# GpSimd in place of ScalarE makes the bfloat16 copy of the adjacency, a step ahead of its use

## The chip, the cores and the metric

The kernel runs on 1 core of one Trainium2 chip. The metric is device time in microseconds of one execution. In this text PE is TensorE, DVE is VectorE, ACT is ScalarE, POOL is GpSimd and SP is SyncE, whose queue issues most of the loads.

## What is computed

The input x has 128 graphs of 128 nodes with 128 features; adj holds for each graph a 128x128 matrix of small integers. Cut to what matters:

```python
h = layernorm(x)
e_k = leaky_relu(einsum('bid,bjd->bij', h * a_k, h), 0.2)     # k = 0..3
alpha = where(adj == k + 1, e_k, alpha)                       # from -9e15, for k = 0..3
x = x + softmax(alpha) @ h
# then, on layernorm(x): 16 experts, top 2 of each token,
# silu(x @ w1[e]) * (x @ w2[e]) @ w3[e], weighted by the gates, added to x
```

## The kernel before

The kernel has two stages. The first walks over the graphs in 32 groups of 4 (T = 4, C = 512 columns) and does the attention and the gating; it ends by sending each token's row to a list in DRAM, sorted by expert. The second reads those lists in tiles of 256 rows and multiplies them with the experts' weights, once for each of the two experts of a token. It isn't touched by the change.

The first stage is written by hand as a software pipeline. `steps(step)` calls a function `step(s, on)` for s = −1 to 33 on each engine, and `on(lag)` is true while group s − lag exists. So in step s the engines work on different groups: the layer norm of group s + 1 (`on(-1)`), the transposed copies and the scores' mask of group s (`on(0)`), its scores on PE a step later (`on(1)`), the softmax (`on(2)`), the new rows (`on(3)`) and the gating (`on(4)`, `on(5)`). Each engine runs its list in order, and semaphores tie them together. What matters here, by engine, in a step s:

- ACT: the first two of the four mask planes, as squares of the adjacency (L677), the copies hT and hTa from PSUM (L685, L687), four exponentials with their sums (L695), then `adjb`, the bfloat16 copy of the adjacency of group s + 1 (L703), x1T (L667), probT (L710), and h of group s + 1 (L716), which waits for the norms (`s_sh`).
- DVE: the maximum of the four scores (L931), statistics of x for group s + 1 (L815), leaky relu (L947), the scaled logits (L846), new rows (L884), the other two mask planes from `adjb` (L966), more statistics (L815) and the top two (L903, L907).
- POOL: `stamp` (two small copies, L545 and L547), `norms_of` (four instructions, L554, L557, L563 with a power, L567), `second_gates` every other step (L573), and from step 7 on `send`, four indirect DMAs of 128 rows each (L581).
- SP: `load_adj` (L387) into one of two int32 buffers, after the squares of two groups before (`s_squares`), `load_x` (L382) into one of six, after the new rows that free it (`s_x1`), and up to step 17 the weights of an expert (`load_expert`).

Before, `adjb` is a single buffer, so ACT writes it for group s + 1 only after DVE has made the mask of group s (`s_pen`). All these areas are slices of one tensor, late, and so the trace calls them late; a row is told by its line.

Of the kernel before, what the change touches and what calls it, by code (L numbers as in the profile page):

```python
# [5 lines left out]
def gnn_then_moe(nc: bass.Bass, x, adj, a0, a1, a2, a3, gate_w, gate_b, w1, w2, w3, out):  # L6
# [7 lines left out]
    f32, bf16, i32, u32, u16 = (mybir.dt.float32, mybir.dt.bfloat16, mybir.dt.int32, mybir.dt.uint32,  # L14
                                mybir.dt.uint16)
# [6 lines left out]
    K = 4  # L22
    T = 4
    G = B // T
    C = T * D
# [3 lines left out]
    ROOT = 2.0 ** 28  # L29
# [49 lines left out]
    with ctx:  # L79
# [18 lines left out]
        score = late[:, K * C:(K + 1) * C]  # L98
        prob = late[:, (K + 1) * C:(K + 3) * C].rearrange("p (q c) -> p q c", q=2)
        adjt = late[:, (K + 3) * C:(K + 5) * C].bitcast(i32).rearrange("p (q c) -> p q c", q=2)  # L100
        adjb = late[:, (K + 5) * C:(K + 6) * C].bitcast(bf16)[:, 0:C]
        pen = late[:, (K + 6) * C:(2 * K + 6) * C].bitcast(bf16).rearrange("p (q k c) -> p q k c", q=2, k=K)
        minusb = sb("minusb", [P, P], bf16)

# [203 lines left out]
        def wait(eng, s, value):  # L308

            if not isinstance(value, int) or value > 0:  # L310
                eng.wait_ge(s, value)
# [13 lines left out]
        def pair(s, lag):  # L325

            return (s - lag) // 2 if 0 < s - lag < G and (s - lag) % 2 else None
# [51 lines left out]
        def _(sp):  # L379
# [4 lines left out]

            def load_adj(g):
                wait(sp, s_squares, g - 1)
                sp.dma_start(adjt[:, g % 2, :].rearrange("p (t d) -> p t d", t=T),  # L387
                             adj_v[:, ds(g * T, T), :]).then_inc(s_adj[g % 2], 16)

# [118 lines left out]
        def _(pool):  # L508
# [41 lines left out]
            def norms_of(s):  # L550
                ln, b = norms(s), s % 2
                wait(pool, s_st1, min(s + 2, G))
                wait(pool, s_st2, s - 3)
                nc.gpsimd.tensor_scalar(veps[:, b, ln, :], stats[:, b, ln, :, 2], 1.0 / D, EPS, ALU.mult, ALU.add  # L554
                                        ).then_inc(s_ve, 1)
                wait(pool, s_sh, s + 1)
                nc.gpsimd.tensor_scalar(negmean[:, ln, :], stats[:, b, ln, :, 1], -1.0, None, ALU.mult  # L557
                                        ).then_inc(s_neg, 1)
                pool.wait_ge(s_ve, s + 2)
                wait(pool, s_h, min(s, G))  # L560
                wait(pool, s_scaled, s - 5)
                wait(pool, s_dest, 2 * (s - 6) + 2)
                nc.gpsimd.tensor_tensor(norm[:, b, ln, :, 0], veps[:, b, ln, :], minus_half[:, ln, :],  # L563
                                        ALU.pow).then_inc(s_rs, 1)
                pool.wait_ge(s_rs, s + 2)
                pool.wait_ge(s_neg, s + 2)
                nc.gpsimd.tensor_tensor(norm[:, b, ln, :, 1], negmean[:, ln, :], norm[:, b, ln, :, 0], ALU.mult  # L567
                                        ).then_inc(s_sh, 1)
# [7 lines left out]
            def send(g, some=range(T)):  # L576
# [3 lines left out]
                for t in some:  # L580
                    pool.indirect_dma_start(  # L581
                        first_list[:, :], bass.IndirectOffsetOnAxis(ap=slot[:, g % SB, t:t + 1], axis=0),
                        stage_v(g % SB)[:, t, :], None).then_inc(s_scat[g % SB], 16)

            def step(s, on):
                if on(5):
                    stamp(s)
                norms_of(s)
                if pair(s, 6) is not None:
                    second_gates(pair(s, 6))  # L590
                if s >= 7 and s <= G:
                    send(s - 7)
# [62 lines left out]
        def _(act):  # L655
# [13 lines left out]
            def step(s, on):  # L669
                b = s % 2  # L670
                if pair(s, 6) is not None:
                    second_gate(pair(s, 6))
                if on(0):
                    act.wait_ge(s_adj[s % 2], (s // 2 + 1) * 16)
                    wait(act, s_S, s - 1)
                    for k in range(SQUARES):
                        last = nc.scalar.activation(pen[:, s % 2, k, :], adjt[:, s % 2, :], ACT.Square,  # L677
                                                    scale=ROOT, bias=shift[:, k:k + 1])
                    last.then_inc(s_squares, 1)
                if s == 0:  # L680
                    act.wait_ge(s_small, 6 * 16)
                if on(0):
                    act.wait_ge(s_hTp, s + 1)
                    wait(act, s_S, s - 1)
                    nc.scalar.activation(hT[:, s % 2, :], psT[:, :], ACT.Copy)  # L685
                    for k in range(K):
                        last = nc.scalar.activation(hTa[s % 2][:, k, :], psT[:, :], ACT.Copy, scale=acol[:, k:k + 1])  # L687
                    last.then_inc(s_hT, 1)
                if on(2):
                    g, p = s - 2, s % 2  # L690
                    act.wait_ge(s_nm, g + 1)
                    wait(act, s_rinv, g - 1)
                    for t in range(T):
                        c = slice(t * D, (t + 1) * D)
                        last = nc.scalar.activation(prob[:, p, c], prob[:, p, c], ACT.Exp,  # L695
                                                    bias=negmax[:, p, t:t + 1],
                                                    accum_out=rowsum[:, p, t:t + 1])
                    last.then_inc(s_prob, 1)
                if on(-1):
                    g = s + 1  # L700
                    act.wait_ge(s_adj[g % 2], (g // 2 + 1) * 16)
                    wait(act, s_pen, g)
                    nc.scalar.activation(adjb, adjt[:, g % 2, :], ACT.Copy).then_inc(s_adjb, 1)  # L703
                if on(4):
                    new_rows_turned(s - 4)
                if on(2):
                    g = s - 2
                    act.wait_ge(s_probTp, g + 1)
                    wait(act, s_O, g)
                    nc.scalar.activation(probT[:, :], psO[:, :], ACT.Copy).then_inc(s_probT, 1)  # L710
                if on(-1):
                    g = s + 1
                    act.wait_ge(s_sh, s + 2)
                    wait(act, s_O, g - HB + 1)
                    for t in range(T):
                        last = nc.scalar.activation(h[:, g % HB, t * D:(t + 1) * D], X[:, g % XQ, t * D:(t + 1) * D],  # L716
                                                    ACT.Identity, scale=norm[:, b, 0, t, 0:1],
                                                    bias=norm[:, b, 0, t, 1:2])
                    last.then_inc(s_h, 1)
# [46 lines left out]
        def _(dve):  # L766
# [157 lines left out]
            def step(s, on):  # L924
# [37 lines left out]
                if on(0):  # L962
                    dve.wait_ge(s_adjb, s + 1)
                    wait(dve, s_S, s - 1)
                    for k in range(SQUARES, K):
                        last = v.tensor_scalar(pen[:, s % 2, k, :], adjb, float(k + 1), ROOT * ROOT,  # L966
                                               ALU.not_equal, ALU.mult)
                    last.then_inc(s_pen, 1)
                if on(3):
# [362 lines left out]
```

## Time and profile before

| | us |
|---|---|
| median of 3 runs | 868.1 (863.27 to 870.77) |
| the profiled execution | 869.26 |
| its span | 867.5 |
| first stage: SP's first load of a list (L446) | at 308.87 |
| POOL busy in the span | 516.5 |
| ACT busy in the span | 416.0 |
| DVE busy in the span | 502.6 |
| PE busy in the span | 732.3 |

A row of the timeline gives the start and the duration in us, the engine, the line of the kernel, the operation, what it writes and reads, and in square brackets the time in which its engine stood idle ahead of it and what ended that. Durations overlap a little, since an engine begins the next instruction before the last one's writes are done, so starts are compared with starts. The profiled execution took 1.8 us more than its span.

### The profile page before, as it was taken

Reading aid. Unit: us, or ns where it says so; the run is one execution under the profiler, and the core shown is the slowest. Engines: PE = TensorE matmul, PEld = TensorE weight load, DVE = VectorE, ACT = ScalarE, POOL = GpSimd, SP = SyncE. Lnnn points to the kernel's source line nnn. Section 1 sums busy time; section 2 is a strip of 40 time slices with the busy share of each in tenths; the row PEclk is TensorE's granted clock in tenths of the full one; section 3 lists DMA queues with packets and bytes.
Section 4 is the critical chain, followed back from the end, with each engine's and each line's share of the span. In section 5 each row is a group of like instructions: output and inputs, shape, how many; then the busy total and the mean of one; then the engine's idle time right before and its main releaser. Section 6 shows DMA issues by size and latency. Waiting matters only on the chain.

```text
span 867.5 us, 17419 instructions
## 1 busy us (share of the span) xinstructions
PE 732.3 (84%) x4422; PEld 588.2 (68%) x4423; DVE 502.6 (58%) x1706; ACT 416.0 (48%) x1011; POOL 516.5 (60%) x670
## 2 busy tenths in 40 slices
PE   4899999999999756888887888886979897988985
PEld 2465656656565645777776888776867787987874
DVE  2899999999999863545444444442433333343332
ACT  7999999999999321222222222222322222222220
POOL 3337777878777766455554554554455554545545
PEclk9999999999999967999999898998999998999998
DMA  5233545332321144776665555534876665566640
GB/s 158 71 112 112 158 121 158 100 104 83 103 85 41 33 152 151 210 232 221 215 224 187 178 176 167 191 122 145 269 214 189 186 192 185 182 183 193 192 140 8
DMA packets 127463, 133.29 MB, mean 154 GB/s; under 512 B 16362, under 2 KB 98545, under 8 KB 127378
## 3 DMA queue, kind: packets, MB, share of 16 engines
q1 hardware_dynamic: 107008, 94.66, 36.6%
q0 software_dynamic: 15616, 34.38, 11.6%
q10 hardware_dynamic: 4754, 3.25, 1.2%
q8 instruction: 36, 0.59, 0.3%
q14 instruction: 49, 0.40, 0.2%
HBM read 52.28 MB, written 41.19 MB: 108 GB/s over the span
## 4 chain that ended last, share of the span: by engine, by line
PE 44%; DVE 23%; issue 16%; another core or an unknown queue 10%; ACT 4%; POOL 1%; DMA 1%; SPq 0%; DVEq 0%; ACTq 0%; POOLq 0%
PE psS L1256 24%; PE bank L1281 14%; PE bank L1271 4%; DVE stage L884 3%; DVE stats L815 3%; DVE late L931 3%; DVE bestix L907 2%; DVE late L947 2%; DVE X L1081 1%; ACT late L687 1%; DVE best L903 1%; DVE late L966 1%; DVE xin L1090 1%; PE psS L1164 1%
## 5 line engine op out<-in xcount | busy, mean ns | idle before, releaser
L1256 PE MATMUL psS<-X,late 128*128 128x256 f32 (+1 forms) x1280 | 262.6, 354 | 3.3 <-issue 3.3
L1081 DVE TENSOR_TENSOR X<-silu,psS 128x512 f32<-128x512 f32 x144 | 98.7, 686 | 225.6 <-remote 132.0
L1256 PEld LDWEIGHTS psS<-X,late 128*128 128x128 f32 x1280 | 212.0, 202 | 22.8 <-issue 3.9
L734 ACT ACTIVATE silu<-psS 128x512 f32<-128x512 f32 x144 | 86.0, 597 | 281.2 <-remote 143.5
L630 POOL DMA_INDIRECT second_list<-xin x144 | 142.1, 987 | 126.0 <-DVE xin L1090 82.4
L641 POOL DMA_INDIRECT out_dram<-xin x144 | 141.7, 984 | 120.7 <-DVE xin L1090 77.4
L1281 PE MATMUL bank<-wts,X 128*128 (+1 forms) x1152 | 164.6, 288 | 36.8 <-DVE X L1081 28.5
L1281 PEld LDWEIGHTS bank<-wts,X 128*128 128x128 f32 x1152 | 147.2, 200 | 46.4 <-issue 46.2
L581 POOL DMA_INDIRECT first_list<-stage,slot x128 | 127.9, 1000 | 52.5 <-issue 41.1
L1090 DVE SCALAR_TENSOR_TENSOR xin<-bank,xin 128x128 f32<-128x128 f32 x288 | 87.5, 345 | 96.7 <-remote 63.3
L1164 PE MATMUL psS<-late,hT 128*128 128x512 f32 x256 | 118.2, 604 | 3.1 <-ACT late L687 2.8
L739 ACT ACTIVATE X<-bank 128x256 f32<-128x256 f32 x144 | 55.2, 383 | 128.0 <-remote 72.0
L1271 PE MATMUL bank<-ident,xin 128*128 128x128 f32 x288 | 58.6, 288 | 44.7 <-issue 39.7
L1271 PEld LDWEIGHTS bank<-ident,xin 128*128 128x128 f32 x288 | 38.8, 148 | 62.5 <-issue 54.8
L1164 PEld LDWEIGHTS psS<-late,hT 128*128 128x128 f32 x256 | 46.9, 194 | 50.1 <-issue 47.2
L931 DVE TENSOR_REDUCE late<-psS 128x512 f32<-128x2048 f32 x32 | 72.9, 2279 | 12.6 <-PE psS L1169 12.1
L687 ACT ACTIVATE late<-bank,acol 128x512 f32<-128x512 f32 x128 | 77.6, 705 | 0.0
L563 POOL TENSOR_TENSOR norm<-veps,minus_half 128x8 f32<-128x8 f32 (+1 forms) x37 | 56.5, 1526 | 0.0
L716 ACT ACTIVATE h<-X,norm 128x128 f32<-128x128 f32 x128 | 53.4, 518 | 1.2 <-POOL norm L567 1.2
L695 ACT ACTIVATE late<-late,negmax 128x128 f32<-128x128 f32 x128 | 50.5, 427 | 6.5 <-DVE negmax L954 6.5
L987 DVE TENSOR_SCALAR xin<-xin 128x128 f32<-128x128 f32 x144 | 44.0, 351 | 0.0
L677 ACT ACTIVATE late<-late,shift 128x512 bf16<-128x512 int32 x64 | 43.4, 742 | 0.0
(156 smaller groups left out, 821.1 us busy)
## 6 DMA issues: line engine op xcount, KB each, us to landing
late<-wts SPq DMA_DIRECT2D x160, 256.0 KB
xin<-second_list SPq DMA_DIRECT2D x48, 262.0 KB
X<-in_x_dram SPq DMA_DIRECT2D x32, 256.0 KB
late<-in_adj_dram SPq DMA_DIRECT2D x32, 256.0 KB
xin<-first_list SPq DMA_DIRECT2D x48, 134.0 KB
xin<-second_list SPq DMA_DIRECT2D x48, 131.0 KB
wts<-in_L_ffn_w_dram SPq DMA_DIRECT2D x48, 128.0 KB
xin<-first_list SPq DMA_DIRECT2D x48, 67.0 KB
```

The costliest lines, as they stand in the source:

```text
L581: pool.indirect_dma_start(first_list[:, :], bass.IndirectOffsetOnAxis(ap=slot[:, g % SB, t:t + 1], axis=0), stage_v(g % SB)[:, t, :], None ...
L630: pool.indirect_dma_start(second_list[:, :], bass.IndirectOffsetOnAxis(ap=xin[:, at, k, SLOT1:SLOT1 + 1].bitcast(i32), axis=0), xin[:, at, ...
L641: pool.indirect_dma_start(out_rows[:, :], bass.IndirectOffsetOnAxis(ap=xin[:, at, k, DEST:DEST + 1].bitcast(i32), axis=0), xin[:, at, k, 0 ...
L687: last = nc.scalar.activation(hTa[s % 2][:, k, :], psT[:, :], ACT.Copy, scale=acol[:, k:k + 1])
L734: nc.scalar.activation(silu[:, u % 2, :], psG[u % 2], ACT.Silu).then_inc(s_silu[u % TURNS], 1)
L931: v.tensor_reduce(score.rearrange("p (t d) -> p t d", t=T), psS[:, :, :].rearrange("p t (k d) -> p t d k", k=K), AX, ALU.max).then_inc(s_s ...
L1081: v.tensor_tensor(hid[:, u % HIDS, :], silu[:, u % 2, :], psU[u % 2], ALU.mult).then_inc(s_hid[u % TURNS], 1)
L1090: last = v.scalar_tensor_tensor(at, psY[k % 2][:, t * D:(t + 1) * D], xin[:, k, t, GATE[r]:GATE[r] + 1], at, ALU.mult, ALU.add)
L1164: mm(psS[:, t, :], hT[:, g % 2, t * D:(t + 1) * D], hTa[g % 2][:, :, t * D:(t + 1) * D], start=True, stop=False)
L1256: last = mm(out[:, c * W2 + rows.start:c * W2 + rows.stop], at[:, half * H + c * P:half * H + (c + 1) * P], xT[:, u % XTS, rows], start=Tr ...
L1271: last = nc.tensor.transpose(psX[k % 2][:, t * P:(t + 1) * P], xin[:, k, t, ROW:ROW2], ident[:, :])
L1281: last = mm(psY[k % 2][:, t * D:(t + 1) * D], hid[:, k % HIDS, at:at + P], wts[:, ds(e[t] * EW + (UP + c * D), D)], start=(c == 0), stop=( ...
```

## The change

POOL makes the copy, as the first work of its step s for group s + 1, into one of two buffers; for group 0 it follows the norms of step −1. ACT's activation goes. `load_adj` waits in addition for the copy of two groups before, since POOL now reads the int32 buffer too. DVE reads the buffer of its group's parity. The two bfloat16 buffers lie where the one lay, in the half of its area that was not used.

```diff
-        adjb = late[:, (K + 5) * C:(K + 6) * C].bitcast(bf16)[:, 0:C]
+        adjb = late[:, (K + 5) * C:(K + 6) * C].bitcast(bf16).rearrange("p (q c) -> p q c", q=2)
...
             def load_adj(g):
                 wait(sp, s_squares, g - 1)
+                wait(sp, s_adjb, g - 1)
...
+            def small_adjacency(g):
+                pool.wait_ge(s_adj[g % 2], (g // 2 + 1) * 16)
+                wait(pool, s_pen, g - 1)
+                nc.gpsimd.tensor_copy(adjb[:, g % 2, :], adjt[:, g % 2, :]).then_inc(s_adjb, 1)
+
             def step(s, on):
+                if on(-1) and s >= 0:
+                    small_adjacency(s + 1)
                 if on(5):
                     stamp(s)
                 norms_of(s)
+                if s < 0:
+                    small_adjacency(0)
...
-                if on(-1):
-                    g = s + 1
-                    act.wait_ge(s_adj[g % 2], (g // 2 + 1) * 16)
-                    wait(act, s_pen, g)
-                    nc.scalar.activation(adjb, adjt[:, g % 2, :], ACT.Copy).then_inc(s_adjb, 1)
                 if on(4):
                     new_rows_turned(s - 4)
...
-                        last = v.tensor_scalar(pen[:, s % 2, k, :], adjb, float(k + 1), ROOT * ROOT,
+                        last = v.tensor_scalar(pen[:, s % 2, k, :], adjb[:, s % 2, :], float(k + 1), ROOT * ROOT,
                                                ALU.not_equal, ALU.mult)
```

On POOL one step of the first stage, with its row sends, stands like this before (stage is the area of the rows to be sent, veps, negmean and norm are the norm's values; the names behind "waits" are semaphores):

```order
L545 COPY stage<-dest 128x4 [waits s_sh]
L547 COPY stage<-norm 128x4x2
L554 TENSOR_SCALAR veps<-stats 128x8 [waits s_st2,s_st1]
L557 TENSOR_SCALAR negmean<-stats 128x8 [waits s_sh]
L563 TENSOR_TENSOR norm<-veps,minus_half 128x8 [waits s_scaled,s_dest,s_h,s_ve]
L567 TENSOR_TENSOR norm<-negmean,norm 128x8 [waits s_neg,s_rs]
L573 TENSOR_TENSOR stage<-e,stage 128x8 [waits s_g1]
```

and like this now (the lines have moved by one, and CAST is the new copy):

```order
L589 CAST late<-late 128x512 [waits s_pen,s_adj0]
L546 COPY stage<-dest 128x4 [waits s_sh]
L548 COPY stage<-norm 128x4x2
L555 TENSOR_SCALAR veps<-stats 128x8 [waits s_st2,s_st1]
L558 TENSOR_SCALAR negmean<-stats 128x8 [waits s_sh]
L564 TENSOR_TENSOR norm<-veps,minus_half 128x8 [waits s_scaled,s_dest,s_h,s_ve]
L568 TENSOR_TENSOR norm<-negmean,norm 128x8 [waits s_neg,s_rs]
L574 TENSOR_TENSOR stage<-e,stage 128x8 [waits s_g1]
```

Everything else of POOL's step now stands behind the copy and its two waits. On ACT the same place before, from the exponentials to h:

```order
L695 ACTIVATE late,rowsum<-late,negmax 128x128 [waits s_rinv,s_nm]
L695 ACTIVATE late,rowsum<-late,negmax 128x128 x3
L703 ACTIVATE late<-late 128x512 [waits s_pen,s_adj1]
L667 ACTIVATE x1T<-bank 128x512 [waits s_L,s_x1Tp]
L710 ACTIVATE probT<-bank 128x512 [waits s_O,s_probTp]
L716 ACTIVATE h<-X,norm 128x128 [waits s_O,s_sh]
```

and now:

```order
L705 ACTIVATE late,rowsum<-late,negmax 128x128 [waits s_rinv,s_nm]
L705 ACTIVATE late,rowsum<-late,negmax 128x128 x3
L677 ACTIVATE x1T<-bank 128x512 [waits s_L,s_x1Tp]
L715 ACTIVATE probT<-bank 128x512 [waits s_O,s_probTp]
L721 ACTIVATE h<-X,norm 128x128 [waits s_O,s_sh]
```

The copy between the exponentials and x1T is gone, and nothing else has moved.

## Rows read from the trace of the kernel before

**Rows 1.** Busy time of each engine, 100 to 260 us, with instruction counts.

```profile
core 0: us, PE busy (x) PEld busy (x) DVE busy (x) ACT busy (x) POOL busy (x), PEclk, DMA share, GB/s
...
100.00:260.00 160.00, 148.72 (x812) 96.24 (x811) 154.27 (x596) 156.79 (x407) 126.39 (x192) 1.00 0.37 109
```

**Rows 2.** Timeline of POOL: step 8, three steps in the middle, step 31.

```profile
73.30 0.20 POOL L545 COPY stage<-dest 128x4 int32<-128x4 int32 x1
...
200.01 0.20 POOL L567 TENSOR_TENSOR norm<-negmean,norm 128x8 f32<-128x8 f32 x1
...
205.65 0.54 POOL L545 COPY stage<-dest 128x4 int32<-128x4 int32 x1
...
209.85 1.15 POOL L581 DMA_INDIRECT first_list<-stage,slot  x1 [0.82 <-POOL stage L573]
211.30 0.96 POOL L581 DMA_INDIRECT first_list<-stage,slot  x1 [0.30 <-issue]
...
214.80 0.46 POOL L545 COPY stage<-dest 128x4 int32<-128x4 int32 x1
...
223.37 0.21 POOL L545 COPY stage<-dest 128x4 int32<-128x4 int32 x1
...
276.47 0.20 POOL L545 COPY stage<-dest 128x4 int32<-128x4 int32 x1
```

**Rows 3.** The stamp's copy in ns (min/median/max), and DVE beside POOL.

```profile
L545 POOL COPY stage<-dest x32: 191/452/606, 41.8 to 319.2; 128x4 int32<-128x4 int32 x32
...
46.91 0.68 DVE L947 SCALAR_TENSOR_TENSOR late<-late 128x512 f32<-128x512 f32 x1
47.08 0.56 POOL L554 TENSOR_SCALAR veps<-stats 128x8 f32<-128x8 f32 x1 [4.98 <-DVE stats L815]
...
205.47 0.68 DVE L947 SCALAR_TENSOR_TENSOR late<-late 128x512 f32<-128x512 f32 x1
206.66 0.23 DVE L846 TENSOR_TENSOR scaled<-bank,norm 128x64 f32<-128x64 f32 x1 [0.52 <-remote]
```

**Rows 4.** Timeline of ACT and PE from the last exponential's sum to h.

```profile
202.30 0.21 ACT L695 ACTIVATION_READ_ACCUMULATOR late<-late,negmax 128x1 f32 x1
202.39 0.63 ACT L703 ACTIVATE late<-late 128x512 bf16<-128x512 int32 x1
202.56 0.66 PE L1179 MATMUL bank<-ident,late 128*128 128x128 f32 x4 [0.57 <-issue]
202.91 0.60 ACT L667 ACTIVATE x1T<-bank 128x512 f32<-128x512 f32 x1
203.39 0.61 ACT L710 ACTIVATE probT<-bank 128x512 f32<-128x512 f32 x1
203.87 1.66 ACT L716 ACTIVATE h<-X,norm 128x128 f32<-128x128 f32 x4
```

**Rows 5.** Timeline of ACT in step 2.

```profile
28.38 0.60 ACT L710 ACTIVATE probT<-bank 128x512 f32<-128x512 f32 x1 [0.23 <-PE bank L1179]
```

**Rows 6.** Timeline of POOL's constants at the start of the kernel.

```profile
1.33 0.54 POOL L516 MEMSET padding<- 128x524 f32 x1
...
3.04 0.20 POOL L532 MEMSET unit<- 1x128 bf16 x1
3.21 0.28 POOL L533 TENSOR_SCALAR_AFFINE_SELECT ident<-ident 128x128 f32<-128x128 f32 x1
3.46 0.28 POOL L535 TENSOR_SCALAR_AFFINE_SELECT lower<-ones 128x128 bf16<-128x128 bf16 x1
```

**Rows 7.** Timeline: POOL's norms of step 31 and DVE's scaled logits of step 32.

```profile
278.49 0.20 POOL L567 TENSOR_TENSOR norm<-negmean,norm 128x4 f32<-128x4 f32 x1
...
285.31 0.22 DVE L846 TENSOR_TENSOR scaled<-bank,norm 128x64 f32<-128x64 f32 x1
```

**Rows 8.** Load of an adjacency, DMA engines busy in 40 slices of 100 to 110 us, POOL's step 12.

```profile
105.27 0.48 SPq L387 DMA_DIRECT2D late<-in_adj_dram  x1
...
DMA  4000000000000000015699995656689999528000
...
108.52 0.45 POOL L545 COPY stage<-dest 128x4 int32<-128x4 int32 x1
```

## The prediction

> **What bounds the kernel now.** I read the busy times by stage first [rows 1]. The change touches only the first stage; the expert tiles behind it keep their code, so they can only start earlier or later. In its steady part, 100 to 260 us, ACT is busy 156.8 of 160 us, DVE 154.3, PE 148.7. POOL shows 126.4, which looks like room. It isn't: the timeline of POOL [rows 2] shows each step's work back to back. The step that begins at 205.65 us is followed by the next at 214.80 and 223.37. Within it nothing waits for another engine; the holes are fixed ones of 0.30 us ahead of each row send (0.8 or 0.5 ahead of the first), which the view calls "issue". They are part of the cost of sending, so POOL's real load is a whole step. From 73.30 us (step 8) to 276.47 us (step 31) 23 steps take 203.2 us, 8.83 each: ACT, DVE and POOL all have about one step of work per step.
>
> What part of POOL's step could give way? Only the first copy of a step, the stamp from dest: its shortest is 0.19 us, its median 0.45 [rows 3]. The reason is in the same group: it starts at 205.65 while DVE runs L947, an instruction with two inputs, and ends at 206.19, just behind DVE's 206.15. The norm chain's first instruction shows the same, 0.56 us instead of 0.20 at 47.08, beside L947 from 46.91 to 47.59. So some 0.26 us a step, 23 × 0.26 = 6.0 us, is stretching and not work. POOL alone would need 203.2 − 6.0 = 197.2 us for these steps, 8.57 each. DVE pays too: L846 starts 0.5 us late at 206.66.
>
> **ACT's part: what is removed.** One activation of 0.65 us a step, start to start 0.52 (202.39 to 202.91), 31 of them besides the first. The trap is what stands around it [rows 4]. The last exponential's sum ends at 202.51. PE can transpose only then, 202.56 to 203.22, and the probability copy L710 needs that. L703 and L667 fill this very hole. Without L703, L667 runs at 202.4 to 203.0, and L710 goes at about 203.24 instead of 203.39. So 0.15 us a step is won, not 0.52. In steps 2 and 3 there is no L667, and L710 waits for PE even now [rows 5]: nothing is won. Only the steps before the first exponential win the whole 0.5. Up to step 7: 0.5 + 4 × 0.15, say 1 us.
>
> **POOL's part: what is added.** One conversion of 128x512 int32 to bf16 ahead of all other work of each step. No row shows it. The nearest is AFFINE_SELECT, which reads and writes 128 elements, 0.25 us start to start (3.21 to 3.46) [rows 6]. If only what exceeds a fixed 0.17 us (the 1x128 memset at 3.04, start to start) grows with size, 512 elements take 0.17 + 4 × 0.08 = 0.5 us; if all of it grows, 1.0 us. The fill of 524 elements took 0.54 without reading anything, so much below 0.5 is out, and a gain from the copy itself is excluded, since POOL did nothing of the kind before. I take the middle, 0.75 us, and keep 0.5 to 1.0; a conversion on a core that runs a program may cost more, so I let 1.3 stand as a tail.
>
> **The sum.** From step 8 POOL would need 8.57 + 0.75 = 9.3 us a step against 8.83 now: it becomes the pace. The stretch goes, since DVE and ACT run ahead to where they wait for POOL, and L947 then stands beside sends and not beside copies. Over 23 steps POOL is late by 23 × 0.75 − 6.0 = 11.3 us, less the 1 us that ACT wins early: 10.3. But POOL's consumers don't feel the first part of that. ACT's h (L716) is what waits for the norms. They are ready at 200.21 and h starts at 203.87 [rows 2, 4]: 3.7 us of slack. DVE and ACT, freed of 0.15 us and of L846's delay, run at some 8.5 and use it up in five or six steps; from there h starts as the norms end. So the stage ends 10.3 − 3.7 = 6.6 us later. In the last steps the same holds for the scaled logits: norms end at 278.69, L846 reads them at 285.31 [rows 7], 6.6 us of slack, of which the drift takes 3.7. Sends that run late aren't waited for by the first tiles, which read only rows of the first 26 groups.
>
> The new waits: the copy waits for its adjacency, and behind it on POOL stand the stamp, the norms and the sends. The load for the group of step 12 is issued at 105.27 and the DMA engines are busy until about 109.2, while POOL's step 12 starts at 108.52 [rows 8]. So in steps that also load weights the copy can wait up to 1 us, at first. The load is released by DVE (L884, the row slot of x), and DVE gets 3.7 us ahead of POOL, so this heals itself; at most 1 or 2 us in all, in the range but not in the sum. The wait for s_pen asks for DVE's step before and is long met. SP's added wait for s_adjb asks for a copy a whole step old: nothing. DVE's pen (L966) gets its input a step earlier, but isn't waiting for it in the steady steps: nothing. Before step 7 POOL sends nothing and waits some 5 us a step for DVE's statistics (4.98 ahead of 47.08, [rows 3]), so its copies there are free.
>
> The profiled execution took 869.3 us (span 867.5). 869.3 + 6.6 = 875.9; the runs' median of 868.1 stands 1.2 below the profile, so I give 875 us.
>
> **A page against the sum.** The rows say that a POOL copy and a two-input DVE instruction do not overlap [rows 3]. The Trainium skill, page "SBUF — State Buffer", section "SBUF: two separate sides", says that the port pair shared by VectorE and GpSimd is an exclusive lock, held for the whole instruction by whoever comes first, against DVE's two-port modes and instructions with two SBUF inputs. By the rows this hits short copies of 0.2 us now; by the rule a long copy would hold DVE out for all its length wherever it meets L947 or L966. The trace agrees with the rule's direction; how long DVE is held by a long copy it can't show. That is the second rival.
>
> **Rivals.** (1) ACT was the bound and POOL hides the copy. For it: ACT is the busiest engine by the count [rows 1]. Then ACT's 0.15 us and part of L846's 0.5 us come back, 0.2 to 0.4 us in each of 30 steps: −6 to −12 us, near 860. Against it: POOL's step has no hole of 0.5 us. It decides only if the copy costs less than 8.83 − 8.57 = 0.26 us, or if the fixed gaps ahead of the sends shrink. (2) The port. The copy (0.75) and DVE's two-input work exclude each other. If POOL drifts so that the copy meets L947 (0.68 us) or L966 (0.5), each copy is stretched by some 0.4 us, or DVE is held for 0.75 and loses what it had over POOL. POOL's step becomes 9.7: 23 × 0.4 = 9 us more, near 884. For it: the present steps meet L947 nearly every time. Against: the meeting place moves by 3.7 us in the first steps, to where DVE does statistics and its top-two search, with one input each, and only L966 is near. A copy of 1.1 us instead of 0.75 gives the same number, 23 × 0.35 = 8 us. (3) The copy is as cheap as the lower price, 0.5 us: 23 × 0.5 − 6.0 − 1 − 3.7 = +0.8 us, no change to be seen.
>
> **Chances.** My forecast (POOL the pace, copy 0.6 to 0.95 us, +3 to +11 us) 0.50; rival 2, with dearer copies, 0.24; rival 3 0.16; rival 1 0.10. About 1% (8.7 us) can be told from no change. Of the forecast two thirds lie within that, a third above; of rival 2 nearly all is above; rival 1 is half inside. That gives slower 0.40, same 0.51, faster 0.09. The range: from 866 (the cheap copy with a little of rival 1) to 886 (rival 2), which leaves out the outer part of rival 1 and copies above 1.2 us.
>
> **What would show it.** The conversion's rows on POOL give its price and the start-to-start to the stamp. In the timeline, stamps should be 9.1 to 9.5 us apart, the stamp's median should fall to 0.2 us, and ACT should be idle ahead of L716 with POOL as the releaser, 0.5 us or more a step; the slack of 3.7 us should be gone by about step 14. DVE's gap ahead of L846 should shrink. L710 should be seen waiting for PE. If instead the norms still end 3 us or more ahead of h at 250 us, my theory is wrong, and if the stamps stay 8.8 apart it is rival 1. If stage two takes another time than before, from its first tile to the end, the difference isn't explained here at all.

## The result and the profile after

| | before | after |
|---|---|---|
| median of 4 runs (lowest to highest), us | 866.5 (863.27 to 870.77) | 880.71 (874.42 to 883.48) |
| profiled execution, its span, us | 869.26, 867.5 | 883.48, 881.8 |
| first list load of the second stage, us from the start | 308.87 | 320.88 |

The changed kernel takes 1.0117 times as long (95% interval 1.0072 to 1.0163): slower by about 10 us (6 to 14), just beyond the 1% that can be told from no change. The medians of the four runs lie 14.2 us apart, at the upper end of that. A second measurement beside its own runs of before gave 1.0116 (1.0020 to 1.0212).

SP issues the first load from the sorted list when the first stage has filled it. It is the best mark of that stage's end, since one profile places it to a fraction of a microsecond while the four runs of after scatter by 9 us. Two profiles of the same kernel differ there by 0.7 us (320.88 and, in again, 321.59). SP's timeline, before and after:

```profile
308.87 0.14 SPq L446 DMA_DIRECT2D xin<-first_list  x1
```

```profile
320.88 0.39 SPq L447 DMA_DIRECT2D xin<-first_list  x1
```

12.0 of the 14.3 us between the two spans arise in the first stage. The 2.3 us left lie in the second, whose code is the same (558.6 and 560.9 us from this load to the span's end); the unchanged kernel's repeat took 552.2 there, so such a difference says nothing.

Busy time of each engine after, 100 to 260 us; it answers to [rows 1]:

```profile
core 0: us, PE busy (x) PEld busy (x) DVE busy (x) ACT busy (x) POOL busy (x), PEclk, DMA share, GB/s
100.00:260.00 160.00, 141.37 (x769) 92.94 (x767) 147.22 (x561) 142.07 (x369) 126.13 (x198) 0.98 0.34 103
```

ACT fell from 156.8 to 142.1 us, more than the copy alone, and DVE and PE fell too. Nobody is at its limit by the count, and POOL's 126 us hide a full step once more. POOL's timeline, two steps, answers to [rows 2]:

```profile
205.15 0.99 POOL L589 CAST late<-late 128x512 bf16<-128x512 int32 x1
206.11 0.18 POOL L546 COPY stage<-dest 128x4 int32<-128x4 int32 x1
...
208.75 0.20 POOL L568 TENSOR_TENSOR norm<-negmean,norm 128x8 f32<-128x8 f32 x1
209.50 1.11 POOL L582 DMA_INDIRECT first_list<-stage,slot  x1 [0.54 <-issue]
...
213.44 0.96 POOL L582 DMA_INDIRECT first_list<-stage,slot  x1 [0.31 <-issue]
214.41 0.62 POOL L589 CAST late<-late 128x512 bf16<-128x512 int32 x1
214.97 0.19 POOL L546 COPY stage<-dest 128x4 int32<-128x4 int32 x1
...
223.72 0.99 POOL L589 CAST late<-late 128x512 bf16<-128x512 int32 x1
```

Three readings. The copy costs 0.56 us from its start to the stamp's (214.41 to 214.97), busy 0.62. The stamp behind it takes 0.18 to 0.20 in every step from 8 to 31: its stretch [rows 3] is gone. And two steps take 18.57 us (205.15 to 223.72), 9.28 each, against 17.72 before (205.65 to 223.37). In every other of these late steps the copy takes 0.99. DVE's timeline shows what it meets there, L952, the two-input instruction that was L947:

```profile
204.64 1.04 DVE L952 SCALAR_TENSOR_TENSOR late<-late 128x512 f32<-128x512 f32 x1
...
213.67 0.68 DVE L952 SCALAR_TENSOR_TENSOR late<-late 128x512 f32<-128x512 f32 x1
```

Where they overlap, both are stretched, DVE's by 0.36 us and the copy by 0.37; neither is held out for the whole of the other. This isn't what makes the kernel slower: in the repeat of the same kernel (again, below) one copy of steps 8 to 31 is stretched so, and it is as much slower than before.

Now the consumers. ACT's timeline from the rows of x1 to h and on to the next hT; it answers to [rows 4]:

```profile
211.03 0.60 ACT L677 ACTIVATE x1T<-bank 128x512 f32<-128x512 f32 x1 [0.45 <-PE bank L1114]
211.53 0.59 ACT L715 ACTIVATE probT<-bank 128x512 f32<-128x512 f32 x1
212.00 1.64 ACT L721 ACTIVATE h<-X,norm 128x128 f32<-128x128 f32 x4
...
215.57 0.60 ACT L695 ACTIVATE hT<-bank 128x512 f32<-128x512 f32 x1 [0.61 <-PE bank L1152]
```

The norms end at 208.95 and h starts at 212.00. The distance is 3.05 us at 209 us and 3.3 at 255, where I had foretold none. ACT waits elsewhere, ahead of hT. The waits from 100 to 260 us, those of PE left out (a wait is put down to the engine that ended it, and to "remote" where the view can name none):

```profile
engine line waited for: us in total, times, longest us
...
DVE scaled L851 <- remote: 11.2, 9, 2.3
ACT hT L695 <- PE bank L1152: 8.6, 13, 0.8
ACT hT L695 <- remote: 4.8, 4, 1.7
...
POOL late L589 <- DMA late<-in_adj_dram: 1.4, 1, 1.4
```

No ACT wait for POOL is among them. TensorE's clock is not what keeps the distance: it was granted 0.98 of full speed here, but 1.00 in the same stretch of again, where the distance is 2.7 to 3.3 us at 180 to 255 us.

DVE's scaled logits wait at the same time. They read the logits of PE's L1143 (PE, then DVE):

```profile
212.00 0.96 PE L1143 MATMUL bank<-gwc,x1T 128*128 128x16 f32 x8
```

```profile
215.42 0.22 DVE L851 TENSOR_TENSOR scaled<-bank,norm 128x64 f32<-128x64 f32 x1 [1.08 <-remote]
```

The logits' matmuls end at 212.96 and the norms at 208.95, and still DVE stands idle for 1.08 us until 215.42. POOL's last send ended at 214.40: the scaled logits start 1.02 us behind it, hT 1.17.

### The profile page after: what moved, and what is told of

It reads as the page before. It is cut to its first block, busy times and chain, and to the rows that moved or that the text cites. A ratio compares the mean times of both kernels' runs of the same rounds, so it can differ in the third digit from the quotient of the medians.

```text
span 881.8 us, 17448 instructions
## 1 busy us (share of the span) xinstructions
PE 733.7 (83%) x4422; PEld 591.2 (67%) x4423; DVE 507.0 (57%) x1706; ACT 402.9 (46%) x979; POOL 532.1 (60%) x702
## 4 chain that ended last, share of the span: by engine, by line
PE 55%; ACT 16%; issue 14%; another core or an unknown queue 8%; DVE 4%; POOL 1%; DMA 1%; SPq 1%; DVEq 1%; ACTq 0%; POOLq 0%
PE psS L1261 23%; PE bank L1286 13%; ACT late L697 6%; PE psS L1169 4%; ACT late L705 4%; PE bank L1276 4%; PE bank L1152 3%; PE bank L1196 2%; ACT h L721 2%; PE bank L1184 2%; PE bank L1143 2%; DVE X L1086 2%; ACT late L687 1%; ACT silu L739 1%
## 5 line engine op out<-in xcount | busy, mean ns | idle before, releaser
L1261 PE MATMUL psS<-X,late 128*128 128x256 f32 (+1 forms) x1280 | 259.8, 351 | 5.8 <-issue 4.1
L1261 PEld LDWEIGHTS psS<-X,late 128*128 128x128 f32 x1280 | 209.8, 200 | 25.5 <-issue 5.3
L1286 PE MATMUL bank<-wts,X 128*128 (+1 forms) x1152 | 166.5, 290 | 30.9 <-DVE X L1086 28.8
L1184 PE MATMUL bank<-ident,late 128*128 128x128 f32 x128 | 20.9, 286 | 27.9 <-ACT late L705 19.6
```

Source lines behind the costliest of these rows:

```text
L1261: last = mm(out[:, c * W2 + rows.start:c * W2 + rows.stop], at[:, half * H + c * P:half * H + (c + 1) * P], xT[:, u % XTS, rows], start=Tr ...
L1286: last = mm(psY[k % 2][:, t * D:(t + 1) * D], hid[:, k % HIDS, at:at + P], wts[:, ds(e[t] * EW + (UP + c * D), D)], start=(c == 0), stop=( ...
```

## The experiments

Eleven more kernels and a repeat of after (again) ran. The table has what their traces show; "8 to 31" is the time from the stamp of step 8 to that of step 31 on POOL, "distance" that from the norms' end to the start of h at about 205 us, "list" the first list load.

| kernel | 8 to 31, us | distance, us | list, us | times before (95%) |
|---|---|---|---|---|
| before | 203.2 | 3.7 | 308.87 | 1 |
| after | 215.0 | 3.1 | 320.88 | 1.0117 (1.0072 to 1.0163) |
| again | 213.7 | 2.7 | 321.59 | 1.0116 (1.0020 to 1.0212) |
| none | 202.0 | 3.5 | 305.56 | 0.9994 (0.9957 to 1.0032) |
| pow_before | 196.7 | 5.1 | 302.20 | 0.9970 (0.9941 to 1.0000) |
| pow_after | 206.6 | 3.4 | 313.39 | 1.0052 (1.0015 to 1.0090) |
| mid | 208.5 | 3.7 | 314.89 | 1.0062 (1.0027 to 1.0098) |
| adjfirst | 210.0 | 3.0 | 315.85 | 1.0133 (1.0046 to 1.0221) |
| dbl | 225.3 | 0.04 | 329.17 | 1.0259 (1.0181 to 1.0337) |
| kick | 218.7 | 0.04 | 319.83 | 1.0177 (1.0136 to 1.0218) |
| stamp_late | 201.4 | 4.1 | 308.58 | 1.0009 (0.9984 to 1.0034) |
| best | 210.7 | 2.4 | 317.03 | 1.0057 (1.0018 to 1.0097) |
| midfirst | 210.0 | 0.04 | 310.85 | 1.0133 (1.0101 to 1.0165) |

nosend moves rows behind the step loop, so its end can't be compared and it has no place in it. Each kernel was measured beside runs of before on its own chip, but the rows of before come from the first chip alone; a list load a microsecond apart on two chips may mean nothing. midfirst's chip was one on which before took 739.56 us. No profile of before was taken there, so it isn't known where before's first stage ends on it.

### none: nobody makes the copy

```diff
-                if on(-1) and s >= 0:
+                if s == 0:
                     small_adjacency(s + 1)
```

(the waits of SP and DVE for the later copies go with them)

> The kernel after, in which nobody makes the bf16 copy of the adjacency behind groups 0 and 1: left out are the copies of groups 2 to 31, so DVE's two pen masks of planes 3 and 4 use old values. It isolates the copy's price on POOL. Theory A (POOL's step is the pace, and the others follow it without the 3.7 us of slack that I counted on): POOL's step falls back by the 0.56 us of the copy to 8.6 to 8.85, the first list load is issued at 307 to 309 us, the time is 865 to 869 in a run whose before is 868. Theory B (the others have a pace of their own and the 12 us come from what the copy does to DVE through the port or to PE's clock): the same fall, but DVE and ACT, freed of both copies, then run ahead of POOL and the stage ends 3 us or more before that of before, time 860 to 864. If neither the copy nor its place matters, 880.

List at 305.56. So taking the copy from ACT is worth some 3.3 us (308.87 to 305.56), and the copy on POOL costs 15.3 (to 320.88). Of the 3.3 us, 1.1 are there at step 8 (72.25 against 73.30) and 1.2 come in steps 8 to 31. The list load lies below Theory A's 307 to 309, where Theory B put it. But B's mechanism isn't seen: DVE and ACT did not run ahead (the distance stayed 3.5), and POOL's step was 8.78 (202.0 / 23), with no wait for another engine in it, within A's 8.6 to 8.85. The time is that of before within its interval.

### pow_before and pow_after: 0.63 us less on POOL

```diff
-                nc.gpsimd.tensor_tensor(norm[:, b, ln, :, 0], veps[:, b, ln, :], minus_half[:, ln, :],
+                pl = slice(0, 1) if 6 <= s <= G - 2 else ln
+                nc.gpsimd.tensor_tensor(norm[:, b, pl, :, 0], veps[:, b, pl, :], minus_half[:, pl, :],
```

> The kernel before with the same cut (left out is the second norm's new rstd in steps 6 to 30). Theory A, in its strong form (before was already paced by POOL's step): stamps 8.2 us apart instead of 8.83, the stage ends up to 15 us earlier, time 853 to 858. If DVE, ACT and PE had a pace of their own near 8.8 in the kernel before: no gain, 866 to 869, and POOL gets waits ahead of its norms. The stretch of the stamp copy beside L947 may change size, 0 to 6 us in either.

> The kernel after, where in steps 6 to 30 the power of the norms is taken for the first norm alone (128x4 instead of 128x8 elements): left out is the second norm's new rstd, which keeps an old value. It takes 1.04 us instead of 1.67, so 0.63 us leave POOL's step, while the copy stays at its place. Theory A: the pace is POOL's, the step falls from 9.28 to about 8.7, the stage ends 25 x 0.63 = 15 us earlier less what another engine's bound gives back; 868 +- 3 us, the copy's loss is gone. Theory B (port or clock at the copy): the copy still meets L952 and the clock, so the time stays at 876 to 881.

Before gained 6.7 us in the list load, not 15. POOL now waits for DVE's statistics ahead of its norms (6.4 us in steps 8 to 31, none in before), and the busy times from 100 to 260 us say who stood next, ACT without a hole:

```profile
100.00:260.00 160.00, 153.21 (x829) 98.31 (x827) 159.02 (x620) 160.00 (x421) 119.38 (x195) 1.00 0.37 111
```

In before POOL was the pace by 0.28 us a step (203.2 − 196.7 = 6.5 over 23), with ACT right behind. After gained 7.5 us in the list load and about half of its lost time (1.0052 against 1.0117); its load waits (5.4 us in 4 times ahead of the copy from 100 to 260 us) took back part of the rest. The expected 868 was too hopeful for a whole return, but the theory that only place and port count (876 to 881) is out.

### mid: the copy behind the norms

```diff
-                if on(-1) and s >= 0:
-                    small_adjacency(s + 1)
                 if on(5):
                     stamp(s)
                 norms_of(s)
-                if s < 0:
-                    small_adjacency(0)
+                if on(-1):
+                    small_adjacency(s + 1)
```

> The kernel after with the copy behind the norms and ahead of the sends of its step, the same work on POOL in another place. The norms, which ACT and DVE wait for, are then not behind the copy of their own step; the sends are. Theory A (the sum of POOL's step is what counts): step 9.3 us, time as after, 878 to 883. Theory A' (what counts is when the sends of a step end, since PE's signals come just behind them): the same as A. The prediction's theory, norms late against h: the norms come 0.6 us earlier once and nothing else changes, so also within 1 us of after. Theory B (the copy beside L952): the copy then stands beside other DVE work, 1 us per pair of steps less, about 12 us in all, 868 to 871.

List 314.89, 6.0 us ahead of after: between A (as after) and B (12 us). The time, 1.0062 of before or 872 us, is nearer to B. POOL's timeline names two sources:

```profile
203.43 0.20 POOL L568 TENSOR_TENSOR norm<-negmean,norm 128x8 f32<-128x8 f32 x1
203.58 0.61 POOL L589 CAST late<-late 128x512 bf16<-128x512 int32 x1
204.37 1.11 POOL L582 DMA_INDIRECT first_list<-stage,slot  x1 [0.17 <-issue]
```

The copy is hardly ever stretched here (0.60 to 0.61, three times 0.66 to 0.70), and in every other step it stands in the fixed gap ahead of the first send, 0.17 us instead of 0.54. In the steps between, L574 stands there and the gap stays 0.82. The same copy costs 0.3 us a step less: (215.0 − 208.5) / 23. By POOL's rows of steps 8 to 31, roughly 4.3 us of the 6.5 are the gaps, 2.0 the waits ahead of the copy, which are gone, and 2.3 the copies' stretch, of which 1.7 comes back as a stretch of the stamp.

### adjfirst: the adjacency loaded ahead of x

```diff
-                if g > 0:
-                    load_adj(g)
-                if g + 2 < G:
-                    load_x(g + 2)
+                if 0 < g < G - 1:
+                    load_adj(g + 1)
+                if 0 < g and g + 2 < G:
+                    load_x(g + 2)
```

(with load_adj(1) ahead of the loop and load_x(2) in its first turn)

> The kernel after, where SP's queue holds the load of the adjacency of group g+1 ahead of the load of x of group g+2, not behind it and the weights. It tells what the copy's wait for its own data costs. If the waits on the landing (62.28, 111.69, 150.01) are on the path: 2 to 4 us earlier first list load, 877 to 879. If they only fill time that the engines get back: no change, 880.7 +- 2. It could also go the other way where x comes later for DVE's statistics.

List 315.85, 5.7 us ahead of again. Step 8 begins 1.6 us earlier, and steps 8 to 31 took 3.7 us less. From step 8 on no wait on the adjacency is left. But these waits were small: POOL's idle time ahead of the copy sums to 1.4 us in again (2.0 in after) over these steps. Most of the other 2.3 us is that POOL's row sends and powers are less stretched: the sends sum to 91.8 us instead of 93.2, the powers to 38.5 instead of 39.2. The copy itself isn't: its mean from 100 to 260 us is 664 ns, against 642 in again. The ratio, 1.0133, can't tell the kernel from after.

### dbl, and again as its reference: the copy twice

```diff
+                wait(pool, s_spare, g)
+                nc.gpsimd.tensor_copy(spare[:, :], adjt[:, g % 2, :]).then_inc(s_spare, 1)
                 nc.gpsimd.tensor_copy(adjb[:, g % 2, :], adjt[:, g % 2, :]).then_inc(s_adjb, 1)
```

> The kernel after once more, unchanged, beside the other runs of this job, so that they have a reference on their own chip. 1.2% above before (95% interval 0.7 to 1.6%), first list load some 12 us later than in before, slack from the norms' end to h 3.1 to 3.3 us at 200 us. It tells no theory from another by itself.

> The kernel after with a second conversion of the same adjacency, into a spare tile, just ahead of the first: 0.6 us more on POOL in each step, nothing else. Theory A (POOL's whole cycle is the pace of all and no slack takes any of it): step 9.85 to 9.9, first list load 25 x 0.56 to 0.6 = 14 us later than in after, time 14 to 15 us above after (894 to 896 if after is 880.7), while h keeps starting about 3 us behind the norms or less by the 0.56 that the norms now come later behind the sends (2.5 us). The prediction's theory (the first 3.7 us are slack and h then starts as the norms end): after has 3.2 us of slack left, so 14 - 3.2 = 11 us, and the slack is gone.

Here my own prediction's mechanism appeared whole. POOL's norms and ACT's h:

```profile
215.71 0.46 POOL L571 TENSOR_TENSOR norm<-negmean,norm 128x8 f32<-128x8 f32 x1
```

```profile
216.21 1.65 ACT L726 ACTIVATE h<-X,norm 128x128 f32<-128x128 f32 x4 [1.87 <-POOL norm L571]
```

h starts 0.04 us behind the norms in almost every step from 98 us on, and ACT waits 14.6 us for POOL between 100 and 260 us. POOL's last stamp but one came 11.0 us later than in again (326.4, 315.4), the list 7.6: the difference, 3.4, is the distance spent. Theory A, no slack at all, is refuted by the list load (7.6 us later, 14 expected) and by the distance, which is gone. The medians agree (10.3 us slower, where A said 14 to 15 and the slack theory 11), but again's four runs scatter by 10 us, so they alone would not decide.

### kick: one delay of 3.3 us

```diff
+                if s == 16:
+                    for k in (0, 8):
+                        nc.gpsimd.tensor_tensor(spin[:, ds(k, 8)], spin[:, ds(k + 16, 8)], spin[:, ds(k + 32, 8)], ALU.pow)
                 if on(5):
                     stamp(s)
```

> The kernel after with one delay: in step 16 POOL does two extra powers of 8 columns (2 x 1.68 = 3.4 us) between the copy and the stamp, and never again. POOL is the pace and late for good by 3.4 us. If the 3 us from the norms' end to h are slack that can be spent once (as the doubled copy shows): h starts as the norms end from step 17 or so on, the first list load comes at most 1 us later than in after (321 to 322.5), the time is that of after. If that distance is kept up by PE's signals behind the last send (as the kernel after shows in steps 8 to 31, where it comes back to 3.2 after each loss): the distance is 3 us again some steps later and the first list load comes 3.4 us later, near 325, time +3 us.

```profile
150.34 3.32 POOL L598 TENSOR_TENSOR spin<-spin 128x8 f32<-128x8 f32 x2
...
202.95 0.20 POOL L570 TENSOR_TENSOR norm<-negmean,norm 128x8 f32<-128x8 f32 x1
```

```profile
203.19 1.65 ACT L726 ACTIVATE h<-X,norm 128x128 f32<-128x128 f32 x4 [0.72 <-POOL norm L570]
```

(POOL, then ACT.) The distance was 3.3 at 142 us, 0.04 at 157, and 0.04 still at 287; only at 184 us was it 1.0 for one step. The first stage's end did not feel the delay: list 319.83, not later than after or again, while POOL's own last stamp came 3.6 to 3.8 us later (334.59 against 330.96 and 330.82). Whether the kernel's time is as free isn't shown: the ratio, 1.0177 (1.0136 to 1.0218), is above that of after, and the intervals overlap. The copy of that step also waited 1.65 us for its adjacency. After has such a wait of 1.38 us in the same step, falls to 1.8 and is back at 3.2 a step later. So but for one delay the same code has two steady states, 3 us apart in h and equal in pace. After stays in the one without a reason that POOL's norms could give.

### nosend: steps without sends

```diff
                 for t in some:
+                    if 8 <= g <= 17:
+                        wait(pool, s_spin, (g - 8) * (T + 1) + t)
+                        nc.gpsimd.tensor_tensor(spin[:, 0:5], spin[:, 8:13], spin[:, 16:21], ALU.pow).then_inc(s_spin, 1)
+                        continue
                     pool.indirect_dma_start(
```

(cut: the rest keeps these rows and their slots, and sends them behind the step loop)

> A look at the steps 15 to 24 (about 140 to 230 us) of the kernel after, where the sends of groups 8 to 17 are left out of their steps: POOL does four powers of five columns in their place (about 5.0 us, and 0.4 for keeping slots and the six last columns), and sends these rows, without their 128 features, behind the step loop. So the end of the run is some 50 us later and only the steps count. Theory S (PE's signals come in one burst 0.9 us behind the last send of a step, and ACT's hT and DVE's scaled logits start from them; that ties all engines to POOL's cycle): in these steps the signals come at their own time, ACT's wait ahead of hT (0.6 us) and DVE's wait ahead of the scaled logits (1.1 to 2.3 us) go, ACT and DVE run ahead at about 8.5 to 8.8 a step until h starts as POOL's norms end: slack 3.2 to 0, and ACT then waits for POOL at h; POOL's own step stays 9.0 to 9.3. Theory N (it is not the sends: the others keep their distance for another reason, a PE chain or the clock): ACT's hT and DVE keep waiting for PE, and the slack stays 3 us.

POOL, ACT and PE in a step without sends:

```profile
192.72 0.20 POOL L582 TENSOR_TENSOR norm<-negmean,norm 128x8 f32<-128x8 f32 x1
192.88 4.90 POOL L598 TENSOR_TENSOR spin<-spin 128x5 f32<-128x5 f32 x4
```

```profile
192.95 1.65 ACT L750 ACTIVATE h<-X,norm 128x128 f32<-128x128 f32 x4 [0.32 <-POOL norm L582]
...
195.83 0.57 ACT L724 ACTIVATE hT<-bank 128x512 f32<-128x512 f32 x1
```

```profile
195.14 0.60 PE L1181 MATMUL bank<-ident,h 128*128 128x128 f32 x4
```

PE's transposes end at 195.74 and hT starts at 195.83, with ACT busy until then (0.41 to 0.44 us behind them in every other step). In the kernel after they end at 214.38 and hT starts at 215.57, with ACT idle for 0.61 us of it; the last send ended at 214.40:

```profile
213.78 0.60 PE L1152 MATMUL bank<-ident,h 128*128 128x128 f32 x4
```

The signs of theory S came: without sends the waits ahead of hT and of the scaled logits are gone from the list of waits from 150 to 230 us, and the distance fell from 3.1 at 147 us to 1.1 at 158, 0.9 at 166 and 0.03 at 193. In the later steps POOL's step was 8.77 (8.92 and 8.62 in turn), shorter than I had set it, and still the others caught up with it. But the run does not isolate the sends. The first 2 us of distance went in a POOL step of 10.2 us (144.30 to 154.48, with the powers, the rows' keeping and 0.7 us of wait for the adjacency), much as in kick; and in kick and midfirst the waits go just so while every send runs. When the sends come back in nosend, the distance stays 0.04. So what is shown is that the waits go with the distance; that the sends are their cause is argued from the times alone.

### stamp_late, best and midfirst: three attempts at a better kernel

stamp_late changes before as follows; best is adjfirst with the same, and with the copy behind the stamps; midfirst is mid and adjfirst together.

```diff
-                if on(5):
-                    stamp(s)
                 norms_of(s)
+                if on(5):
+                    stamp(s)
```

> The kernel before (ACT makes the copy) with the two stamp copies of a POOL step moved behind the norms, ahead of the sends. Nothing is left out. The first stamp then doesn't stand beside L947 (0.26 us a step of stretch) and fills part of the gap of 0.5 us ahead of the first send. If POOL's step is the pace in before too: step 8.83 down to 8.5, where ACT becomes the bound; first list load 302 to 305 instead of 308.9, as where the power was cut (302.2); time 3 to 6 us below before. If not: 308 +- 1, no change.

> The kernel after put together from what the runs showed: the adjacency's load ahead of that of x, and on POOL the norms first, then the two stamp copies, then the conversion, then the sends. Nothing is left out. In mid the conversion behind the norms took 0.3 us a step less than at the step's head (no meeting with L952, and part of the fixed gap of 0.5 us ahead of the first send filled), adjfirst took the landing waits away. With the stamps there too, theory: POOL's step 8.8 or less, first list load 308 to 312, time within 1% of before (+0 to +4 us). If the send's gap is a cost of its own that nothing can fill and the stamps' place is of no account: step 9.0, list load 313 to 315, +5 to +7 us.

> mid and adjfirst together: POOL's order is that of mid (stamps, norms, conversion, sends), and SP loads the next adjacency ahead of x. Nothing is left out. If the two gains add up (mid 6 us earlier first list load than after, adjfirst 5.7 us in its job): first list load 309 to 311, time 0 to 3 us above before. If the landing waits were already hidden in mid (no wait on the adjacency is seen there from 100 to 260 us): 313 to 315, +4 to +6 us as mid. It would not beat the kernel before by either.

stamp_late gained nothing in the list load (308.58), though POOL's steps 8 to 31 took 1.7 us less: the stretch beside DVE moved on to POOL's next instructions. L554, first of the norms, takes some 0.43 us in most steps instead of 0.20, and in every other step the power takes 1.99 instead of 1.68.

```profile
197.50 1.99 POOL L563 TENSOR_TENSOR norm<-veps,minus_half 128x8 f32<-128x8 f32 x1
...
200.45 1.11 POOL L581 DMA_INDIRECT first_list<-stage,slot  x1 [0.42 <-POOL stage L547]
```

best missed its 308 to 312 (list 317.03); here some sends themselves were stretched, from 0.96 to 1.23 or 1.40 us, which I can't explain. midfirst met 309 to 311 with 310.85, and yet lost to its before by 1.33%, 10 us, where 0 to 3 were expected; as before has no profile on that chip, the list load doesn't say where they arise. Its distance went 2.2, 2.1, 0.65, 0.22 and was spent by 113 us, without a kick. None of the three beats before.

## Why the prediction was right, and where it wasn't

The forecast was 875 us, slower by a little, range 866 to 886; the median is 880.7, inside the range. Of the three outcomes I had given most to a change within 1%; it came out just beyond, on the slower side, where the second largest chance stood. Term by term:

- **POOL becomes the pace: right.** Foretold 9.3 us a step, measured 9.28 in the late steps and 9.35 over all 23 (9.29 in again); dbl and the two pow kernels show that the stage follows POOL's step.
- **Price of the copy: too high.** 0.75 taken, 0.56 measured, inside the 0.5 to 1.0. Between the stamps of steps 8 and 31 stand 22 copies and not 23, since step 31 makes none: 22 × 0.19 = 4.2 us too much, and 0.75 for the copy too many.
- **The stretch vanishes (−6.0): right for the stamp,** 0.18 to 0.20 us in all these steps. But six copies of the late steps met L952 and grew by 0.4, 2.3 us in all: rival 2 in small, at the place that I had argued it would leave. In again one did.
- **Landing waits outside the sum, 1 to 2 us: the size was right,** 2.0 us ahead of the copy in after and 1.4 in again. The healing that I counted on did not come, since DVE never got the 3.7 us ahead: one wait of 1.4 us is as late as 150 us.
- **POOL late by 11.3 us: 11.8 measured** (215.0 − 203.2). The rows give 22 × 0.56 = 12.3 for the copies, 6.1 less for the stamp's stretch, and 2.3 for the stretched copies, 2.0 for the waits and 1.1 for longer sends: 11.6. So the agreement is luck: 5.0 us too much for the copies cancel against 5.4 that the sum didn't have.
- **The early gain of ACT, 1 us:** DVE's maximum of step 7 starts at 60.06 instead of 61.21, but at the first send POOL stands where it stood (73.25 and 73.30). Nothing of it is left. In none, where POOL makes no copies in the steps before, step 8 does begin 1.1 us early (72.25), so the gain was sized rightly and POOL's early copies and their waits took it. Over the whole stage ACT's part was worth 3.3 us (none).
- **The failed step: "3.7 us of slack that DVE and ACT use up in five or six steps; from there h starts as the norms end."** The distance was still 2.9 to 3.4 at 200 to 255 us. The stage ends 12.0 us later, not 6.6: the early gain and the slack were both subtracted and neither was to be had. By my own test (norms 3 us ahead of h at 250 us) this part of the theory is wrong for this kernel. The reason is not that the slack is unreal; dbl, kick, nosend and midfirst spend it. In after DVE and ACT are held, step by step, at two places whose inputs come from PE: hT and the scaled logits start about 1 us behind POOL's last send, after PE has done its part (the logits 2.5 us before), and they move with the send when POOL's step grows. A sign of it stood in rows 3. I put the 0.52 us ahead of L846 down to the stretch beside the stamp and counted it as freed. By its place it is this same wait: in before L846 starts 1.0 us behind a last send too, in the step ahead (197.42) the stamp is stretched and L846 waits for nothing, and in after, where no stamp is stretched, it is up to 2.3 us. What holds them is open: no view shows it, nosend does not isolate the sends, and it depends on the phase, since in kick, behind the delay, the same sends run and no wait ahead of hT is in the list of waits.
- **L710's wait for PE:** the 0.15 instead of 0.52 us was a fair reading; ACT waits 1.6 us for PE ahead of probT from 100 to 260 us and 13.4 ahead of hT (8.6 for PE, 4.8 "remote"), so ACT's freed time was never in short supply.
- **The rule on the shared port** (the Trainium skill, page "SBUF — State Buffer", section "SBUF: two separate sides": an exclusive lock, the other side held out) had the right partners. What they do to each other differs. L952 began first, at 204.64, and takes 0.68 us alone; by the rule it would have ended undisturbed at 205.32 and kept the copy, begun at 205.15, out for 0.17. Measured, both were longer, DVE by 0.36 us and POOL by 0.37. Here the measurement decides.

## What to carry to other kernels

An engine whose busy share is 79% can be the pace, if its holes are fixed gaps of its own instructions: read its timeline step to step, and a copy moved there costs its start-to-start time in each step. Idle distance between a producer and its consumer is slack only if nothing else holds the consumer; look at what the consumer waits for ahead of that instruction, and whether that moves along with the producer. Here that wait was in the rows before the change, half a microsecond every other step. Where an instruction must be added to such an engine, put it in a fixed gap (here behind the norms, ahead of the sends: 0.3 us a step less) and bring its data earlier. Neither made the move pay here: of the kernels with the copy on POOL and nothing left out, none was faster than before.

## What the runs showed of the hardware that I had not expected

- In the phase that before and after keep, ACT and DVE get PE's results about 1 us behind the end of POOL's last indirect DMA of a step (hT 1.17 and the scaled logits 1.02 us behind it at 215 us), though PE was done 1.19 and 2.46 us before they started. Where the distance is spent (kick, midfirst, dbl) or no sends run (nosend), hT starts within 0.52 us of PE's transposes and ACT doesn't wait ahead of it. That the sends do it isn't shown.
- Two steady states at one pace: a single delay of 3.3 us on the pacing engine moved its consumers from 3.3 us behind the norms to 0.04 for nearly all the rest of the stage, and the stage's end came no later (319.83 against 320.88 and 321.59).
- A conversion of 128x512 int32 to bf16 takes POOL 0.56 us start to start, at the cheap end of the 0.5 to 1.0 that the 128 elements in 0.25 [rows 6] had given, and about what filling 524 elements takes (0.54); two in a row in dbl took 0.56 each.
- The gap ahead of the first send shrinks from 0.54 to 0.17 us when a copy stands in front of it, so it is not a cost of the send alone. Behind L574, which the send needs, it stays 0.82.
